# Attention with a planned order: TensorE's products written out as tables, value products in runs, four probability buffers

## What is computed

```python
c_q = x @ W_dq
Q = (c_q @ W_uq).reshape(Bx, Sx, N_HEADS, D_K)
c_kv = x @ W_dkv
K = (c_kv @ W_uk).reshape(Bx, Sx, N_HEADS, D_K)
V = (c_kv @ W_uv).reshape(Bx, Sx, N_HEADS, D_K)
scores = jnp.einsum('bqhd,bkhd->bhqk', Q, K) / math.sqrt(D_K)
scores = jnp.where(causal, scores, -jnp.inf)
attn = jax.nn.softmax(scores, axis=-1)
out = jnp.einsum('bhqk,bkhd->bqhd', attn, V).reshape(Bx, Sx, N_HEADS * D_K)
return out @ W_o
```

## Time and profile before

| | us |
|---|---|
| median of 3 runs | 1239.85 (1236.3 to 1243.09) |
| profiled execution | 1230.27 |
| its span | 1228.5 |
| TensorE matmuls busy | 1047.3 (85% of the span) |
| TensorE weight loads busy | 634.7 (52%) |
| VectorE busy | 829.1 (67%) |
| ScalarE busy | 666.9 (54%) |
| GpSimd busy | 384.3 (31%) |

### The profile page before, as it was taken

The page is one execution under the profiler, slowest core; times in us unless marked ns, Lnnn a source line. Parts: engine busy times, 40 slices in busy tenths (PEclk is TensorE's granted clock), DMA queues, the critical chain, the costliest instruction groups (busy, mean ns, idle before and its releaser), DMA issues. The chain is left out here.

```text
span 1228.5 us, 22512 instructions
## 1 busy us (share of the span) xinstructions
PE 1047.3 (85%) x6988; PEld 634.7 (52%) x6988; DVE 829.1 (67%) x2536; ACT 666.9 (54%) x1672; POOL 384.3 (31%) x404
## 2 busy tenths in 40 slices
PE   4439999993997999999999999999869369999960
PEld 2228888881442434443444444444347248888850
DVE  7774444436979888888888888888147754444428
ACT  5604555552771666666666666667646315555530
POOL 6516777762011000000000000000048236777740
PEclk9659999996996999999999999999989759999985
DMA  8402333326955344444444444440147112333338
GB/s 332 169 9 94 102 102 104 105 86 234 264 200 103 53 62 62 62 63 62 63 62 63 62 63 62 63 62 11 47 161 256 46 39 95 104 104 103 104 123 353
DMA packets 75200, 132.52 MB, mean 108 GB/s; under 512 B 29712, under 2 KB 42448, under 8 KB 75088
## 3 DMA queue, kind: packets, MB, share of 16 engines
q1 hardware_dynamic: 60304, 89.65, 30.1%
q0 software_dynamic: 13632, 37.24, 8.9%
q10 hardware_dynamic: 1152, 4.19, 0.8%
HBM read 82.42 MB, written 48.23 MB: 106 GB/s over the span
## 5 line engine op out<-in xcount | busy, mean ns | idle before, releaser
L1418 ACT ACTIVATE all_expert_rows<-stacks_bank 128x512 f32<-128x512 f32 (+3 forms) x768 | 326.4, 494 | 167.7 <-PE stacks_bank L1350 144.6
L1433 DVE CUSTOM_DVE_ANT_0 stacks_bank<-stacks_bank,all_causal 128x128 f32<-128x128 f32 (+3 forms) x512 | 245.3, 504 | 35.4 <-PE stacks_bank L1321 31.6
L1436 DVE TENSOR_REDUCE t_maxp<-stacks_bank 128x1 f32<-128x512 f32 x256 | 175.5, 685 | 22.9 <-PE stacks_bank L1321 22.4
L1321 PE MATMUL stacks_bank<-stacks_kst,stacks_qst 96*128 96x512 bf16 (+2 forms) x528 | 157.6, 345 | 10.2 <-DVE t_maxp L1433 4.6
L1361 PE MATMUL stacks_bank<-all_expert_rows,stacks_turned_or_values 128*32 128x512 f32 (+3 forms) x1536 | 163.6, 498 | 2.7 <-ACT all_expert_rows L1418 0.7
L615 POOL DMA_INDIRECT y_rows<-all_expert_rows,all_slot x142 | 140.0, 986 | 53.1 <-issue 39.6
L1347 PE MATMUL stacks_bank<-stacks_qst,stacks_kst 99*128 99x512 bf16 (+3 forms) x528 | 154.5, 333 | 2.2 <-ACT all_expert_rows L1418 1.5
L1299 POOL COPY stacks_turned_or_values<-stacks_values 128x512 f32<-128x512 f32 x16 | 9.8, 612 | 426.7 <-DMA stacks_kst<-qk_parts 284.6
L1321 PEld LDWEIGHTS stacks_bank<-stacks_kst,stacks_qst 96*128 96x128 bf16 x528 | 47.9, 98 | 127.4 <-DVE t_maxp L1433 66.6
L655 PE MATMUL ae_psG<-a_w,ae_xT 128*128 x426 | 111.8, 398 | 0.0
L655 PE MATMUL be_psG<-b_w,be_xT 128*128 x426 | 111.5, 398 | 0.0
(11 more groups left out here) (295 smaller groups left out, 1823.1 us busy)
## 6 DMA issues: line engine op xcount, KB each, us to landing
all_expert_rows<-y_rows SPq DMA_DIRECT2D x32, 512.0 KB, 7.5
stacks_qst<-qk_parts SPq DMA_DIRECT2D x66, 128.0 KB, 4.7
stacks_kst<-qk_parts SPq DMA_DIRECT2D x66, 128.0 KB, 7.1
stacks_parts_or_stacks<-qk_parts SPq DMA_DIRECT2D x60, 128.0 KB, 5.8
a_w<-in_experts SPq DMA_DIRECT2D x8, 768.0 KB, 8.1
qk_parts<-stacks_parts_or_stacks SPq DMA_DIRECT2D x16, 384.0 KB, 2.7
qk_parts<-q_parts SPq DMA_DIRECT2D x16, 384.0 KB, 3.7
b_w<-in_experts SPq DMA_DIRECT2D x8, 768.0 KB, 6.2
```

The lines of the kernel that those rows point to most:

```text
L1321: nc.tensor.matmul(psR[bank][:, 0:w], qst[slot][0:KROWS, h, i * P:(i + 1) * P], kst[slot][0:KROWS, h, k0:k0 + w], start=True, stop=True).t ...
L1418: nc.scalar.activation(prob[j % 2][:, h, a:(c + 1) * 512], psS[n % ST_BANKS][:, a - c * 512:512], ACT.Exp, scale=DK ** -0.5).then_inc(exp_ ...
L1433: ins = nc.vector.tensor_tensor_reduce(psR[bank][:, 0:w], psR[bank][:, 0:w], T.causal[:, 512 - w:512], 1.0, -BIG, ALU.add, ALU.max, maxp[: ...
L1436: ins = nc.vector.tensor_reduce(maxp[:, h, col:col + 1], psR[bank][:, 0:w], AX_X, ALU.max)
```

## The change

`plan_step` no longer plans. `ORDERS` holds four strings, one letter for each piece of work, and TensorE, VectorE and now ScalarE follow them. Value products stand in runs of one to four. The probability memory, the same in size, is cut into four buffers of one half each (`PROBS`), used in turn by block number, so that a block's first exponential waits for the product of the block four before it. The wait for the maxima stands before the step's first column score in place of the step's start. ScalarE copies the output at the place of its last product in the order.

```diff
--- before.py
+++ after.py
@@ -69,8 +69,7 @@
 ST_BANKS = 3
 AHEAD = 11
 FIRST_AHEAD = 5
-M_BEHIND = 3
-READER_LATENCY = 1000
+PROBS = 4
 Y_BUFS = 4
 Y_EARLY = Y_BUFS - 1
 Y_LOADED = 16 * TOPK * (NT // U // Y_BUFS)
@@ -1113,69 +1112,34 @@
     return units
 
 
+ORDERS = {
+    (2, False): ("tsststststststsvstsstsvssttststssttsvtsstststsvssttsstts"
+             "tsvttstststtstssvsstststtsstsvvssttmstststvvststtstststt"
+             "svv"),
+    (2, True): ("sttsststststototssttssttssttsvvststststsvsststtstststsvs"
+             "ttsststttsvtsstststtsstsvvstsstmttststsvvvsttstststtsvv"),
+    (1, True): ("tstststsststvtsstststststtstsvstsststtsvsttststtsststvst"
+             "ststtstssttsvvstststtststottvtmttvttotttvvvv"),
+    (0, True): ("tttottttvtttotttvtttvtttttttvtttvtttttvttttvttvtttvtttvt"
+             "ttttvv"),
+}
+
+
 def plan_step(units, later, with_before):
 
 
 
 
-
     width = lambda j, c: min((c + 1) * 512, S) - max(c * 512, j * P)
-    ring = [("s", u, 1) for u in range(AHEAD if with_before else FIRST_AHEAD, len(units))] if later else []
-    after = [("s", u, 2) for u in range(AHEAD)] if later > 1 else []
-    if later:
-        ring += after[:M_BEHIND] + [("m", 1)] + after[M_BEHIND:]
-    if with_before:
-        at = 4 if later else 0
-        ring[at:at] = [("o", c) for c in range(2)]
-    st = [("st", j, c, h) for j in range(QT) for c in range(2) for h in range(HG) if width(j, c) > 0]
-    pv = [("pv", j, c) for j in range(QT) for c in range(2) if width(j, c) > 0]
...
-            pv_end[j, c] = t + 150
-            order.append(pv[n_pv])
-            n_pv += 1
+    scores = [("s", u, 1) for u in range(AHEAD if with_before else FIRST_AHEAD, len(units))] if later else []
+    scores += [("s", u, 2) for u in range(AHEAD)] if later > 1 else []
+    blocks = [(j, c) for j in range(QT) for c in range(2) if width(j, c) > 0]
+    of_letter = {"s": scores, "t": [("st", j, c, h) for j, c in blocks for h in range(HG)],
+                 "v": [("pv", j, c) for j, c in blocks], "m": [("m", 1)] if later else [],
+                 "o": [("o", c) for c in range(2)] if with_before else []}
+    letters = ORDERS[later, with_before]
+    assert all(letters.count(letter) == len(work) for letter, work in of_letter.items())
+    order = [of_letter[letter][letters[:at].count(letter)] for at, letter in enumerate(letters)]
     return order, [x for x in order if x[0] in "smo"]
 
 
@@ -1197,7 +1161,7 @@
     qst, kst, loaded, N_LOADS = A.qst, A.kst, A.loaded, A.N_LOADS
     one = QT * HG * VW
     vst = [A.turned_or_values[:, s * one:(s + 1) * one].rearrange("p (j w) -> p j w", j=QT) for s in range(SLOTS)]
-    prob = [A.rows_or_prob[:, i * (HG * S):(i + 1) * (HG * S)].rearrange("p (h t) -> p h t", h=HG) for i in range(2)]
+    prob = [A.rows_or_prob[:, i * (HG * 512):(i + 1) * (HG * 512)].rearrange("p (h t) -> p h t", h=HG) for i in range(PROBS)]
     maxp = M.sb("maxp", [P, HG, QT + QHALF])
     maxq = M.sb("maxq", [P, HG, QT])
     neg, mid = M.sb("neg", [MROW, P]), M.sb("mid", [MROW, P])
@@ -1216,7 +1180,7 @@
     CHAIN = 4
     plans = {(later, with_before): plan_step(units, later, with_before)
              for later, with_before in {(min(2, NG - 1 - g), g > 0) for g in range(NG)}}
-    assert RING % RING_BANKS == 0 and ST % ST_BANKS == 0
+    assert RING % RING_BANKS == 0 and ST % ST_BANKS == 0 and PV % PROBS == 0
 
     def steps(step):
 
@@ -1359,15 +1323,16 @@
                 wait(pe, o_copied, g * 2 + c - 1)
             for h in range(HG):
                 ins = nc.tensor.matmul(psO[c][h * VW:(h + 1) * VW, a - c * 512:512],
-                                       vst[k][:, j, h * VW:(h + 1) * VW], prob[j % 2][:, h, a:(c + 1) * 512],
+                                       vst[k][:, j, h * VW:(h + 1) * VW], prob[n_pv[j, c] % PROBS][:, h, a - c * 512:512],
                                        start=(j == 0), stop=(j == QHALF * (c + 1) - 1))
             ins.then_inc(pv_done, 1)
 
         def step(g, k, later, with_before):
             base, idx, asked = ring_base(g), 0, False
-            pe.wait_ge(m_loaded, g * (16 * PARTS) + 16 * PARTS)
             for what, *at in plans[later, with_before][0]:
                 if what == "st":
+                    if at == [0, 0, 0]:
+                        pe.wait_ge(m_loaded, g * (16 * PARTS) + 16 * PARTS)
                     score_t(g, k, *at)
                     continue
                 if what == "pv":
@@ -1406,20 +1371,17 @@
             nc.scalar.copy(oT[:, c, :], psO[c][:]).then_inc(o_copied, 1)
 
         def step(g, k, later, with_before):
-            for (j, c), n in n_pv.items():
-
-                if j > 1:
-                    act.wait_ge(pv_done, g * PV + n_pv[j - 2, c] + 1)
-                else:
-                    wait(act, pv_done, (g - 1) * PV + n_pv[j + QHALF * (c + 1) - 2, c] + 1)
-                for h in range(HG):
-                    n, a = n_st[j, c, h], max(c * 512, j * P)
+            for what, *at in plans[later, with_before][0]:
+                if what == "st":
+                    j, c, h = at
+                    block, n, a = n_pv[j, c], n_st[j, c, h], max(c * 512, j * P)
+                    if h == 0:
+                        wait(act, pv_done, g * PV + block + 1 - PROBS)
                     act.wait_ge(st_done, g * ST + n + 1)
-                    nc.scalar.activation(prob[j % 2][:, h, a:(c + 1) * 512], psS[n % ST_BANKS][:, a - c * 512:512], ACT.Exp,
+                    nc.scalar.activation(prob[block % PROBS][:, h, a - c * 512:512], psS[n % ST_BANKS][:, a - c * 512:512], ACT.Exp,
                                          scale=DK ** -0.5).then_inc(exp_done, 1)
-                if j == QHALF + 1:
-                    copy_out(g, 0)
-            copy_out(g, 1)
+                elif what == "pv" and at[0] == QHALF * (at[1] + 1) - 1:
+                    copy_out(g, at[1])
 
         T.prepare(ACT.Exp, TOPK)
         act.wait_ge(Q.low_ready, Q.CH * Q.NU)
```

More of the change, by code:

```diff
@@ L1131, in plan_step @@
-    pv = [("pv", j, c) for j in range(QT) for c in range(2) if width(j, c) > 0]
[L1132 to L1172, removed]
-        else:
-            _, j, c = pv[n_pv]
-            t = start + width(j, c) * 4 / 2.4
-            pv_end[j, c] = t + 150
-            order.append(pv[n_pv])
-            n_pv += 1
```

## The result

The changed kernel takes 1193.22 us (median of 4 runs, 1191.74 to 1194.76), the kernel before 1238.07 (4 runs, 1229.75 to 1243.09): ratio 0.9624, 95% interval 0.9592 to 0.9655. The forecast was 1216 with a range of 1206 to 1231: the direction held, the gain was about twice what I had worked out.

What follows compares the result with a forecast made beforehand. TensorE was taken to set attention's pace, with about 1.4 us of waits per 30.72 us group. Terms 13.1 + 3.9 + 3.0 + 0.7 + 3.0 = 23.7 us off the 1239.85 median gave 1216 us, range 1206 to 1231.

Steps and rivals of the forecast that it cites:

- Joints: Product blocks in runs on TensorE: 73 joints saved at 0.18 us each, 13.1 us (6.6 to 17.5).
- Rival 1: A joint in a run costs as much as a switch, so 13.1 us goes to nothing: 1229 us; chance 0.17.
- Order of the rest: TensorE's waits in groups 1 to 13 fall from 1.4 to 1.0-1.1 us a group: 3.9 us gained.
- Rival 4: Nearly all waits go, a group at 28.6 in place of 29.5 us: 1204 us; chance 0.10.
- Rival 2: VectorE runs dry behind long runs and TensorE waits for banks, a group at 31.8 us: 1248 us; chance 0.07.
- Four buffers: Exponentials get room across all blocks; worth nothing by itself in steady groups, but the runs couldn't be without it.
- Maxima earlier: Waits for the maxima's DMAs at the starts of groups 1 to 13 go: 3.0 us gained.
- Group 14 to 15: TensorE's 2.87 us wait ahead of group 15 shrinks to 2.2 behind SyncE's in-order queue: 0.7 us gained.
- Last group: Later products in the last group end waits between TensorE and ScalarE: 3.0 us gained (1.5 to 5).

Runs made afterwards that it cites:

- run 5: Changed kernel with the products of groups 1 to 13 in four runs of three instead of seven runs: 1238.1 us, ratio 1.001 to the kernel before.
- Run 3: Changed kernel with products of groups 1 to 13 one by one, each three column scores behind the last it needs: 1259.7 us, ratio 1.018 to the kernel before.
- run 1: Changed kernel with the old planner's four orders in ORDERS, all else kept: 1242.5 us, ratio 1.003 to the kernel before.
- Run 11: Changed kernel with group 14's two output transposes moved early, after 11 and 14 pieces of work: 1192.2 us, ratio 0.965 to the kernel before.

## Why the prediction was wrong

**Joints (13.1 us forecast, 17.2 measured).** The run of three in the changed kernel, TensorE's timeline; each row of x4 is a pass of four heads:

```profile
602.09 0.64 PE L1325 MATMUL stacks_bank<-all_expert_rows,stacks_turned_or_values 128*32 128x512 f32 x4
...
602.54 0.61 PE L1325 MATMUL stacks_bank<-all_expert_rows,stacks_turned_or_values 128*32 128x512 f32 x4
...
602.97 0.61 PE L1325 MATMUL stacks_bank<-all_expert_rows,stacks_turned_or_values 128*32 128x512 f32 x4
...
603.40 0.61 PE L1325 MATMUL stacks_bank<-all_expert_rows,stacks_turned_or_values 128*32 128x512 f32 x4
```

The first pass is 0.45 ahead of the second, as in the earlier trace rows; from there each step is 0.43, which is 2 x 512 columns at 2.4 GHz: a second block costs 0.86 us where a single one cost 1.00 and 0.09 to enter. So a joint saves 0.235, the upper of the bounds that I had kept (0.24), and 73 of them 17.2 us. I had taken the pass to pass step of 0.45 for the joint; it holds only for the first block of a run. Rival 1 is dead.

By the Trainium skill (TensorEngine Tiling (Array Packing), Key Properties) a change of tiling mode drains TensorE, and a change of tile alone does not. The trace agrees, as a joint inside a run takes no longer than a step inside a block (0.43). That the 0.235 are such a drain and nothing else is not shown: the transpose of the maxima has 128*32 in its record too, and it costs nothing to enter and no more than its columns to leave:

```profile
600.49 0.22 PE L1314 MATMUL stacks_bank<-all_causal_t,all_ident_bf 128*128 128x128 bf16 x1
600.55 0.27 PE L1298 MATMUL stacks_bank<-all_ident,t_maxq 128*32 128x128 f32 x1
600.66 0.33 PE L1311 MATMUL stacks_bank<-stacks_qst,stacks_kst 99*128 99x384 bf16 x1
```

**Order of the rest (3.9 forecast, about 15.7 measured).** This is the step that failed. A steady group lost 2.38 us, of which five joints are 1.18: 1.2 us of waits went, 13 times. Of these some 0.7 were ahead of row scores, 0.3 ahead of column scores and 0.2 ahead of a product. I had left 1.0 to 1.1 us of waits in a group, 0.5 of it in the segment sststtstststsv. Here is that segment's start and end on TensorE, and VectorE around it:

```profile
588.74 0.38 PE L1285 MATMUL stacks_bank<-stacks_kst,stacks_qst 96*128 96x512 bf16 x1
589.05 0.85 PE L1325 MATMUL stacks_bank<-all_expert_rows,stacks_turned_or_values 128*32 128x384 f32 x8
589.84 0.45 PE L1285 MATMUL stacks_bank<-stacks_kst,stacks_qst 96*128 96x128 bf16 x2
...
592.05 0.38 PE L1285 MATMUL stacks_bank<-stacks_kst,stacks_qst 96*128 96x512 bf16 x1
592.36 1.07 PE L1325 MATMUL stacks_bank<-all_expert_rows,stacks_turned_or_values 128*32 128x512 f32 x8
```

```profile
588.87 0.73 DVE L1395 CUSTOM_DVE_ANT_0 stacks_bank<-stacks_bank,all_causal 128x512 f32<-128x512 f32 x1
589.51 0.14 DVE L1395 DVE_READ_ACCUMULATOR2_ANT t_maxp<- 128x1 f32 x1
589.51 0.68 DVE L1398 TENSOR_REDUCE t_maxp<-stacks_bank 128x1 f32<-128x512 f32 x1
590.12 0.29 DVE L1395 CUSTOM_DVE_ANT_0 stacks_bank<-stacks_bank,all_causal 128x128 f32<-128x128 f32 x1
```

When the product starts at 589.05, VectorE has not three full banks before it but the rest of one score and one more: it is through at 590.12, 0.28 us after the product's end. I had reckoned with 1.1 left over, three scores less the product. With 0.3 the sum comes out without a wait, and so it is: 589.84 to 592.36 is 2.52 us for 2.42 of work and 0.09 to enter. The assumption that the ring is full at each run's start was wrong, and it is what left 0.5 us here, and the other waits were left "likewise". Over the seven runs of a steady group three banks were taken at the start of three and two at the start of four, and VectorE was through 1.0 to 1.3 us after the start, only behind the maxima 2.0; three scores are 1.5 to 2.1. Rival 4 (a group at 28.6) had it nearly right at 0.10; 28.34 is below even that.

What the runs add: fit matters more than either part. The same runs in another order, or the same order with other runs, have 3.4 and 4.5 us of waits. Rival 2 therefore isn't a phantom: run 5 shows its mechanism, 5.8 us of idle VectorE and 31.85 us for a group where its price was 5.2 and 31.8, only not in this table. Run 3 waits for VectorE's banks too but has no run at all, so it isn't rival 2's case.

**Four buffers.** Worth nothing alone (run 1, ratio 1.003), as forecast. That the tables can't do without them was only argued and not tried.

**Maxima earlier (3.0 forecast).** The late starts of groups 1, 5 and 12 were 0.4, 1.1 and 1.0 us long before; after, no group starts late, and only group 6 has a wait of its own, 0.3 us for ScalarE five us into its step: 2.2 us.

**Group 14 to 15 (0.7 forecast).** The mechanism held to the step:

```profile
829.42 0.60 PE L1304 MATMUL stacks_bank<-all_ident,stacks_left_or_out 128*128 128x128 f32 x4
...
830.06 0.44 DVE L1434 COPY t_orow<-stacks_bank 128x272 f32<-128x272 f32 x1 [0.77 <-PE stacks_bank L1304]
...
830.53 0.57 SPq L1215 DMA_DIRECT2D o_rows<-t_orow  x1
831.14 1.91 SPq L1221 DMA_DIRECT2D stacks_qst<-t_mparts  x3
834.34 0.39 PE L1311 MATMUL stacks_bank<-stacks_qst,stacks_kst 99*128 99x512 bf16 x1 [1.66 <-DMA stacks_qst<-t_mparts]
```

The store of group 13's rows stands ahead of the maxima in SyncE's queue, and TensorE stands 1.66 us where I had 2.2, and 2.87 before. Run 11 shows the cause, and that the rest costs little: without it the steps are only 0.25 us shorter. **Last group (3.0 forecast):** 27.1 to 23.3, of which 0.24 is its joint: 3.6. That it is the later products that did it was not tried alone. Group 0, for which I had only three joints (0.7), lost 1.95.

Sum in the traces: 17.2 + 15.7 + 2.2 + 3.6, 1.25 in group 0 and 1.8 in group 14 with the wait behind it, besides joints: 41.7, against 41.5 measured. The 44.9 between the medians lean on four executions of each kernel: against 42 later executions of the kernel before, in three sets with medians of 1236.9, 1235.9 and 1236.6, the changed kernel is 42.7 to 43.6 faster, close to attention's 41.5. What stays open: why executions of one kernel spread so much ahead of attention, and how much of run 3's loss is the splitting and how much the moving.

## What to carry to other kernels

When one engine is fed from rings of few banks, an order is good or bad as a whole: nearly the same work took 28.34, 31.52, 31.85 or 33.78 us here. Grouping the long pieces that need no bank paid only in the order made for it; in the old order it cost 0.4 us a group, although it saved 1.2 in switches. In a forecast, don't set every buffer full at the start of each stretch: follow the reader's backlog from stretch to stretch. The waits that this forecast left in by such an assumption (11.8 us) were two thirds of what it missed. And price a joint from its bounds on both sides; the nearest row was the pessimistic one.

## What was unexpected of the hardware

In a run of float32 products with four heads in 32 columns each, the second and later blocks have no gap for the change of weights between their two passes: the step is 0.43 us for 512 columns where the first block's is 0.45. The first pass to pass step of a run is the only one that is longer, by 0.024 us at every width (0.134 against 0.109 at 128 columns, 0.240 against 0.216 at 256, 0.347 against 0.322 at 384, 0.453 against 0.429 at 512).
